# Third edge loop of a four-layer graph network: TensorE makes one unread identity product in the next piece's bank before it waits for that piece's operands

## The reference

```python
def _L2_gnn_ref(h, src, dst, rel_type, norm, bases, w_comp):
    ...
    weight = jnp.einsum('rb,bio->rio', w_comp, bases)      # 32 relations from 8 bases
    xw = jnp.einsum('ni,rio->nro', h, weight)
    msg = xw[src, rel_type] * norm
    out = jax.ops.segment_sum(msg, dst, num_segments=h.shape[0])
    return jax.nn.relu(out)
```

## Time and profile before

| | |
|---|---|
| median of 3 runs | 8210.89 us (8205.14 to 8220.28) |
| profiled execution | 8210.32 us |
| its span | 8208.5 us |
| mean granted TensorE clock | 0.782 |
| PE busy | 5486.4 us (67%) |
| DVE busy | 5435.7 us (66%) |
| POOL busy | 3711.2 us (45%) |
| ACT busy | 2562.7 us (31%) |

### The profile page before, as it was taken

The page is one execution under the profiler, slowest core; times in us unless marked ns, Lnnn a source line. Parts: engine busy times, 40 slices in busy tenths (PEclk is TensorE's granted clock), DMA queues, the critical chain, the costliest instruction groups (busy, mean ns, idle before and its releaser), DMA issues.

```text
span 8208.5 us, 116030 instructions
## 1 busy us (share of the span) xinstructions
PE 5486.4 (67%) x23622; PEld 4033.4 (49%) x23625; DVE 5435.7 (66%) x13161; ACT 2562.7 (31%) x9014; POOL 3711.2 (45%) x3988
## 2 busy tenths in 40 slices
PE   6365666526666666975555555799677777777798
PEld 4133333313433333434555555688455555555587
DVE  9767666766767664226655555675578777777666
ACT  1022222302222221112444444311345544545211
POOL 0267666536666662343555555200244444444211
PEclk8576676666667777986777777899788888888899
DMA  3232333323333331023333333355355454544411
GB/s 105 54 87 84 87 88 87 86 78 93 87 92 86 95 88 48 31 75 102 108 107 106 105 106 106 107 158 164 97 139 138 136 140 134 139 138 138 95 44 36
DMA packets 427643, 820.10 MB, mean 100 GB/s; under 512 B 75880, under 2 KB 275544, under 8 KB 426458
## 3 DMA queue, kind: packets, MB, share of 16 engines
q0 software_dynamic: 194048, 574.45, 25.2%
q1 hardware_dynamic: 230618, 231.98, 9.1%
q10 hardware_dynamic: 2304, 6.29, 0.3%
HBM read 692.86 MB, written 279.19 MB: 118 GB/s over the span
## 4 chain that ended last, share of the span: by engine, by line
PE 27%; DVE 17%; issue 10%; another core or an unknown queue 5%; SPq 3%; DMA 2%; ACT 1%; DVEq 1%; ACTq 1%; POOL 0%; POOLq 0%
PE ps L1482 4%; PE ps L1747 3%; DVE big L1417 3%; SPq L1340 2%; PE ps L1710 2%; PE ps L1936 2%; PE ps L1953 2%; DVE big L1840 2%; PE ps L831 2%; DVE big L1856 2%; DMA bas_d<-big 2%; PE ps L1432 2%; DVE big L1865 2%; DVE wreg L1828 1%
## 5 line engine op out<-in xcount | busy, mean ns | idle before, releaser
L831 PE MATMUL ps<-ring 128*128 x3528 | 1574.4, 578 | 1114.1 <-issue 478.5
L831 PEld LDWEIGHTS ps<-ring 128*128 128x128 f32 x3528 | 758.8, 266 | 1583.3 <-issue 1556.4
L1432 PE MATMUL ps<-big,ring 128*128 128x128 f32 x4928 | 885.2, 347 | 628.4 <-DVE big L1407 431.2
L745 POOL DMA_INDIRECT ring<-xl_d,idx x832 | 843.2, 1013 | 737.2 <-DVEq L640 316.3
L812 ACT CAST ring<-ohb 128x128 f32<-128x128 bf16 x1764 | 523.5, 298 | 2075.8 <-DVE ohb L775 1266.5
L1432 PEld LDWEIGHTS ps<-big,ring 128*128 128x128 f32 x4928 | 806.6, 251 | 707.0 <-DVE big L1407 486.5
L1368 POOL DMA_INDIRECT big<-x_d,idx x832 | 793.0, 953 | 790.6 <-ACT ring L1393 545.4
L1618 POOL DMA_INDIRECT ring<-kv_d,gidx x754 | 712.7, 945 | 841.5 <-issue 758.3
L745 POOL DMA_INDIRECT ring<-x_d,idx x832 | 825.9, 993 | 443.3 <-issue 225.4
L785 DVE TENSOR_TENSOR big<-big,ps 128x257 f32 (+1 forms) x1764 | 754.6, 428 | 259.1 <-issue 187.8
L1417 DVE SCALAR_TENSOR_TENSOR big<-big,ps 128x256 f32<-128x256 f32 x1232 | 590.1, 479 | 369.1 <-DMA bas_d<-big 210.1
(11 more groups left out here) (408 smaller groups left out, 9157.4 us busy)
## 6 DMA issues: line engine op xcount, KB each, us to landing
bas_d<-big SPq DMA_DIRECT2D x1232, 128.0 KB
att_d<-wreg SPq DMA_DIRECT2D x464, 132.0 KB
big<-bas_d SPq DMA_DIRECT2D x49, 1024.0 KB, 5.6
x_d<-ring SPq DMA_DIRECT2D x147, 128.0 KB, 1.7
ring<-xl_d,idx POOLq DMA_INDIRECT x832
ring<-x_d,idx POOLq DMA_INDIRECT x832
big<-x_d,idx POOLq DMA_INDIRECT x832
kv_d<-ring SPq DMA_DIRECT2D x49, 260.0 KB, 2.3
```

The costliest lines, as they stand in the source:

```text
L745: nc.gpsimd.indirect_dma_start(out=rows[:, j, :], out_offset=None, in_=table, in_offset=bass.IndirectOffsetOnAxis(ap=idx_of(c), axis=0)).t ...
L831: T.matmul(ps[k][:, 0:D], ohf[:, k, :], rows[:, slot, :].rearrange("p a d -> p (a d)"), start=True, stop=True)
L1432: last = nc.tensor.matmul(ps[j % 8][:, 0:FW].rearrange("p (n h b) -> p n h b", n=NB, h=H)[:, :, h, :], xs[:, j, h * P:(h + 1) * P], wts[:, ...
```

## The change

From the ninth piece on, PE's wait for the bank (`l2_cur`) moves ahead of its waits for weights and rows, and behind it stands one new product of the identity matrix with itself into columns 256 to 383 of the same bank. A piece's sum takes columns 0 to 255, so nobody reads the new columns, and the new product counts no semaphore. There are 1,224 such products in the loop.

```diff
         def l2_edges_pe(pe):
             def step(c, j, i):
+                if past(c, 8):
+                    pe.wait_ge(l2_cur, c - 7)
+                    nc.tensor.matmul(ps[j % 8][:, FW:FW + P], ident[:, :], ident[:, :], start=True, stop=True)
                 pe.wait_ge(l2_w, c + 1)
                 pe.wait_ge(l2_x, c + 1)
-                if past(c, 8):
-                    pe.wait_ge(l2_cur, c - 7)
                 for h in range(H):
                     last = nc.tensor.matmul(ps[j % 8][:, 0:FW].rearrange("p (n h b) -> p n h b", n=NB, h=H)[:, :, h, :],
                                             xs[:, j, h * P:(h + 1) * P], wts[:, j % 8], start=True, stop=True)
```

## The result

The changed kernel takes 8241.58 us, the median of five runs (8238.86 to 8246.91); the kernel before took 8205.14 us in the five runs beside it (8201.54 to 8220.28). The ratio is 1.0042, with a 95% interval of 1.0027 to 1.0057: the change costs 36 us. The profiled execution took 8239.25 us.

The account below looks back on a forecast made before the run. The prediction took the loop to be a ring of waits with no engine full and SP a near second limit. The profiled 8210.3 us plus 11 us for ACT's waits, other terms 0, gave 8221 us, range 8190 to 8270.

Parts of the forecast that it names:

- Within 0.2%: Whole kernel: outcome of no measurable change, about 16 us either way; given a chance of 0.50.
- The signs of being wrong: Loop: accumulations waiting for PE over 50 us, length over 1530 or under 1495 us, or a changed number of gather gaps.
- The product itself: PE in the loop: each new product takes 0.31 us in the mean, all 1,224 together 379 us.
- What lies in waits: PE in the loop: products at 258 waits cost nothing if the bank is free; the other 966 lengthen streams by 299 us.
- The moved wait: PE's bank wait, one product earlier: costs nothing; 13 us at most if the bank comes free last.
- The clock: PE's clock in the loop: at most 38 us of gain where products are hidden; taken as 0.
- the third rival: Loop: identity products bridge short waits and hold the clock, up to 38 us faster, 8172 us; chance 0.13.
- The chosen sixth of 69 us: ACT's 54 waits for PE in the loop: of at most 69 us added, one in six was taken, 11 us.
- PE becomes the bound: Loop: PE limits at today's clock mix with no slack, 68 us slower, 8279 us; chance 0.27.
- two groups at half clock: PE in the loop: two successive groups with products take 10.2 us against DVE's 6.3, so slack runs out.
- Counts miss the batch: PE's counts slip into POOL's next gather batch; one in fifteen slipping costs 65 us, 8276 us; chance 0.10.
- The end of the loop: Last 64 pieces, without gathers: products add 14 us of PE time, hidden at 52.5 of 56 us; otherwise some 4 us.

Follow-up runs that it names:

- e8: Two bf16 identity products ahead of each piece in place of the change's one 32-bit product; against the kernel before, ratio 1.0068, 56 us more.
- e9: The change's 32-bit identity product with 256 columns in place of 128; against the kernel before, ratio 1.0080, 65 us more.
- e6: The change's identity product placed behind all three waits, in the order of the kernel before; against the kernel before, ratio 1.0064, 51 us more.
- e11: No identity product; each piece made by one product of 256 columns, its sum left transposed; against the kernel before, ratio 0.9946, 41 us less.
- e12: Each piece made by one product of 256 columns, sum transposed, with the change's identity product ahead; against the kernel before, ratio 1.0005, 7 us from before.
- e3: Only the bank wait moved ahead, no identity product; against the kernel before on a quicker chip, ratio 1.0000, 7075.78 us.
- e5: The changed kernel run again, on a chip like that of the first measurement; against the kernel before, ratio 1.0064, 8169.89 us for 8112.65.
- e10: The change's 32-bit identity product cut to 8 columns, on a chip where the kernel before takes 8112 to 8118 us; ratio 1.0138, 122 us more.
- e1: The change's identity product cut from 128 to 8 columns, on the quicker chip; against the kernel before, ratio 1.0070, 7122.68 us for 7069.61.
- e4: Two 32-bit identity products ahead of each piece, on the quicker chip; against the kernel before, ratio 1.0105, 76 us more.
- e7: One bf16 identity product ahead of each piece in place of the 32-bit one; against the kernel before, ratio 1.0018, 17 us more.

## Why the prediction came out as it did

- **Direction and range.** A small loss was forecast, 8221 us with a range of 8190 to 8270 us; 8241.58 us lies in it. Against the kernel before it is 36 us where 11 were forecast: three times as much. "Within 0.2%" was held likeliest, and the loss is 0.42%. That the time fell in the range is partly luck: the range was made for other causes than the one that the runs show.
- **The signs of being wrong.** The loop was forecast at 1507 to 1523 us and took 1529, just under the 1530 named. Two signs did come: DVE's accumulations waited for PE for 52.0 us, over the 50 named, and the runs of gathers went from 111 to 122, most of the added ones being runs of eight that broke into fours.
- **The step that failed** is "The product itself", which priced the product by its records' time in the array, and "What lies in waits", which gave 258 of them for nothing. The array time was about right: line 1429 has the 2,448 records, and PE is busy for 1093 us in the loop where 1143 were forecast (line 1429 alone shows 558.4 us, over the 250 to 400 forecast, since its records' modelled ends lie over the records behind them). But it is not what costs: half of it (e8) or twice it (e9) costs nearly the same, and a product made outside of the waits (e6) costs the same as one inside. The four entries per piece cost, at the end of POOL's runs of gathers. e11 and e12 show it in the other direction.
- **What was seen and not followed.** The prediction read out of the earlier trace rows that counts travel slowly in a batch, and that SP's stores take 2.0 us in place of 0.50. It applied this to counts and to SP, not to how PE comes by its instructions.
- **The moved wait** was priced at nothing: right by e3, on the chip where gathers hold nobody up, and by e6 beside e5 where they do, as far as the two can be told apart.
- **The clock** was priced at nothing: right as to the time. It rose from 0.78 to 0.82, as forecast, and returned nothing; e8 has 0.78 and loses as much as e5, e9 has 0.89 and loses no less. The Trainium skill ("TensorE: Matmul & The Clock Gate", "Why this matters for your kernels") advises to leave TensorE no long idle gaps, which the third rival weighed. The clock did rise here, and the kernel got 36 us slower. e10 shows the opposite case, which the prediction thought hardly possible: a busier PE with a granted clock of 0.54.
- **ACT's waits for PE** grew by 191 us, where 20 or more were forecast. The chosen sixth of 69 us was too little, and the cause given for it, a group at half clock, is not the one in the timeline.
- **The rivals.** "PE becomes the bound" is nearest in what the profile shows, with 61% of the chain on PE, but its cause, two groups at half clock, is not what the timeline shows; the price of 68 us was nearer to the 52 to 57 us of e5 than to the first measurement's 36. "Counts miss the batch" is part of it: ACT's waits of up to 9.1 us for PE. In the stretch shown they come from PE's slow supply rather than from a group that ends 1.3 us later.
- **The end of the loop** was forecast as just hidden, with 52.5 us of PE time: it has 52.13 us busy in 58 us, and took 2 us more.

Left open: why PE's and SP's instructions come at 0.7 us while POOL issues gathers on some chips, and not on the one of e1 to e4, so that the slow supply itself is read from the traces and not made or taken away by an experiment; why two entries (e7) cost less than half of four; what makes the clock fall in e10; and why the same change costs 0.42% on one chip and 0.64% on another, whose intervals just overlap. A kernel with e11's piece and a next stage that takes transposed sums was not built, so its 41 us are what the loop gives, before the cost of that stage.

## What to carry to other kernels

Filler products for an idle TensorE are not free because they fit into its waits: count them as entries in its list too, and look whether the engine has stretches of "issue" time with its operands ready, while another engine issues gathers. If it has, fewer and wider instructions can gain where less array work does not: here two products of 128 columns made into one of 256 gained 41 us. And look who waits for whom before making an engine busier: a clock that rose from 0.78 to 0.82 returned nothing here.

## What the runs showed of the hardware

- Where the kernel before takes 8112 to 8205 us, SP's instructions come slowly in the loop: in the ten traces from there 564 to 870 of its some 4,000 records start 0.65 to 0.80 us after the one before, and in the batch of the earlier trace rows a store took 2.0 us in place of 0.50. With eleven or thirteen entries per piece PE has 57 to 431 such starts. On the chip of e1 to e4, where the kernel takes 7070 us, SP has 21 to 48 and PE 0 to 26, and e3's loop ran in 1024 us where the loop before took 1507 on the first chip.
- A 32-bit product of 128 x 128 by 128 columns stands in the trace as two loads and two multiplications, 0.111 us apart at full clock and 0.211 us at half; in bf16 it is one of each, 0.056 us at full clock (e8).
- PE busy for 1518 of 1580 us with a product of 8 columns ahead of each piece was granted a clock of 0.54 (e10), where the product of 128 columns had 0.82 at 1093 busy us of 1529.
